# How the weights' sums of a cross attention are laid out, and who divides by them: one decoder layer on one NeuronCore

## The chip, the cores and the metric

The kernel runs on one core of one Trainium2 chip. The metric is the device time of one execution in microseconds (us). The core's engines run side by side, each through its own list of instructions in order: TensorE (PE in the profile; PEld is its loading of stationary operands), VectorE (DVE), ScalarE (ACT), GpSimd (POOL) and SyncE (SP), which issues the DMAs. They wait for each other on semaphores. TensorE writes into eight banks of PSUM (128 x 512 floats each) and the others read them.

## The reference

One layer of a decoder for x of 2048 x 256 and a context of 1601 x 256, all in float32:

```python
x = x + self_attention(layernorm(x))          # 16 heads of 16, causal, ALiBi
x = x + cross_attention(layernorm(x), ctx)    # 16 heads of 64, below
x = x + fp8_gemm(layernorm(x))                # 256 x 256
# cross attention
q, k, v = query @ Wq + bq, ctx @ Wk + bk, ctx @ Wv + bv
attn = softmax(q k^T / 8)                     # over the 1601 keys, for each head
out = concat_heads(attn @ v) @ Wo + bo + query
out = layernorm(out) * gamma + beta
```

## The kernel before, in words

A class `Order` writes one list of stages by hand; every engine's program walks through this list and does its own part of each stage. What stands later in the list comes later on every engine, and a wait of one instruction holds everything behind it on its engine. The method `after(steps, what)` puts a stage into the list a number of steps of the attention later.

The change is in the cross attention. Its 16 heads go in 8 pairs (`NP`), a pair is computed for 4 blocks of 512 queries (`NB`), and a block in 13 steps of 128 keys (`NS`; the last has 65). So there are 32 blocks and 416 steps. In a step TensorE makes the scores of both heads with keys on the partitions and queries in the row (L842 and L846), ScalarE writes their exponentials, the weights, from PSUM to SBUF (L1001), and TensorE multiplies them with the values (L857): head 0 into partitions 0 to 63 and head 1 into 64 to 127 of one bank, so `products` holds head, feature x query. The two heads' matmuls of a step stand one behind the other and use different columns of the array. The weights are kept in 12 buffers, six steps' worth.

The softmax needs the sum of the weights over all keys. GpSimd adds the 13 weight tiles of each head up into `added` (L1348, 24 additions of 128x512 a block, lagging behind the steps). Four steps after a block's end (`SUMS_LAG`) TensorE adds over the partitions: 8 matmuls, each with a 128x128 piece of `added` as the stationary operand and a column of ones moving (L868), which gives the sums as columns, queries on the partitions. VectorE takes the reciprocal of these 8 columns (L1186). Four steps later (`PROJECT_LAG`) TensorE projects the products, copied to `o_pair` by ScalarE (L1011), with Wo: per head and per 128 queries a matmul of 64 rows (L880), heads in separate banks since each still has to be divided by its own sums, four banks in all. VectorE reads them in 8 instructions of 128x256, each multiplying by the reciprocals and adding to the residual `resid` (L1204).

Beside the steps of one pair, TensorE does the work ahead for the next: projections (L664, L818) and 64 chunks of scores (L830, two banks each), from which VectorE takes the row maxima (L1107). All of this, the sums and the projection share a ring of three banks (`CROSS_RING`); `take_bank` waits until the bank used three uses ago has been read. The last pair (p = 7) has no such side work. There the tail of the layer (L1233 to L1274: the layer norms, rounding to fp8, the last product) runs between the steps, block by block, behind each block's projection (`TAIL_AT`), mostly on VectorE, with the small powers for the norms on GpSimd (L1310, L1312).

## Time and profile before

| | |
|---|---|
| median of 3 runs | 2216.82 us (2206.26 to 2250.86) |
| the profiled execution, its time | 2230.43 us |
| its span, first to last instruction | 2228.5 us |
| mean granted TensorE clock | 0.911 |
| cross attention | about 748 to the end |
| its last pair | about 2007 to the end |

The page gives each engine's busy time as a share of the span, and in 40 slices as tenths. The views behind it follow an engine in a stretch of time: what it ran, how long it sat idle before each group of instructions, and who ended that idle time.

### The profile page before, as it was taken

The numbers are of one execution on the slowest core, as the hardware profiler recorded it, in microseconds if no ns is written. First come the engines' busy times: TensorE is split into PE (matmuls) and PEld (weight loads), VectorE is DVE, ScalarE is ACT, GpSimd is POOL, SyncE is SP. The second block draws the span as 40 slices with busy tenths as digits, with TensorE's granted clock in tenths as the row PEclk, the third lists the DMA queues.
The fourth block names the chain that finished last, engine by engine and source line by source line (L and its number), as shares of the span: only waits on it lengthen the run. The fifth ranks groups of instructions, "written<-read, shape, count | busy, mean of one in ns | idle before, by whom it ended". The sixth has DMA issues, their size and how long they took to land.

```text
span 2228.5 us, 32080 instructions
## 1 busy us (share of the span) xinstructions
PE 1964.8 (88%) x11994; PEld 1069.0 (48%) x11994; DVE 1247.4 (56%) x2495; ACT 879.5 (39%) x1762; POOL 1027.2 (46%) x856
## 2 busy tenths in 40 slices
...
GB/s 103 26 31 30 30 16 17 31 92 1 11 38 29 8 1 8 1 1 10 1 1 11 1 1 11 1 1 10 1 1 3 1 1 3 1 26 3 1 19 38
DMA packets 27746, 34.63 MB, mean 16 GB/s; under 512 B 3986, under 2 KB 25811, under 8 KB 25939
## 3 DMA queue, kind: packets, MB, share of 16 engines
...
q14 instruction: 59, 0.48, 0.1%
...
## 4 chain that ended last, share of the span: by engine, by line
PE 75%; DVE 11%; issue 6%; ACT 4%; POOL 2%; SPq 1%; DMA 1%; POOLq 0%; DVEq 0%; ACTq 0%
PE psum L857 17%; PE psum L842 12%; DVE maxima L1107 7%; PE psum L830 7%; PE psum L750 7%; PE psum L664 5%; PE psum L725 5%; PE psum L698 4%; PE psum L846 4%; ACT weights_room L943 3%; PE psum L880 3%; PE psum L818 2%; PE psum L868 2%; PE psum L762 2%; PE psum L734 1%
## 5 line engine op out<-in xcount | busy, mean ns | idle before, releaser
L1107 DVE TENSOR_REDUCE maxima<-psum 128x1 f32<-128x400 f32 (+5 forms) x1664 | 882.4, 583 | 456.9 <-PE psum L830 276.9
L1348 POOL TENSOR_TENSOR parts_room<-parts_room,weights_room 128x512 f32<-128x512 f32 (+1 forms) x596 | 746.8, 1286 | 339.1 <-ACT weights_room L1001 339.0
L1001 ACT ACTIVATE weights_room<-psum 128x512 f32<-128x512 f32 (+1 forms) x694 | 370.0, 597 | 610.6 <-PE psum L846 608.7
L943 ACT ACTIVATE weights_room<-psum 128x512 f32<-128x512 f32 (+3 forms) x640 | 298.0, 535 | 253.6 <-PE psum L725 136.5
L1310 POOL TENSOR_SCALAR rstd<-meanvar 128x2 f32<-128x2 f32 (+1 forms) x24 | 6.7, 280 | 701.9 <-DVE meanvar L1057 701.9
L842 PE MATMUL psum<-stack_room,k_hi 64*128 64x512 f32 (+1 forms) x1664 | 304.0, 411 | 9.3 <-ACT weights_room L1001 7.7
L830 PE MATMUL psum<-k_hi,stack_room 64*128 64x400 f32 (+1 forms) x1024 | 254.3, 404 | 37.0 <-DVE maxima L1107 34.8
L830 PEld LDWEIGHTS psum<-k_hi,stack_room 64*128 64x128 f32 x1024 | 145.5, 189 | 215.3 <-issue 124.3
L725 PE MATMUL psum<-stack_room,stack_room 51*128 51x512 f32 (+3 forms) x640 | 203.7, 458 | 41.1 <-ACT weights_room L943 39.9
L842 PEld LDWEIGHTS psum<-stack_room,k_hi 64*128 64x128 f32 (+1 forms) x1664 | 167.8, 185 | 59.6 <-issue 29.2
L846 PE MATMUL psum<-shifts,parts_room 64*128 64x512 f32 (+1 forms) x832 | 189.8, 395 | 0.0
L842 PE MATMUL psum<-stack_room,k_lo 64*128 64x512 f32 (+1 forms) x832 | 189.8, 395 | 0.0
L698 PE MATMUL psum<-stack_room,stack_room 51*128 51x512 f32 (+3 forms) x640 | 170.3, 494 | 19.2 <-DVE maxima L1107 13.1
L857 PE MATMUL psum<-weights_room,parts_room 128*64 128x512 f32 (+1 forms) x696 | 185.0, 644 | 0.0
L857 PE MATMUL psum<-weights_room,v_pair 128*64 128x512 f32 (+1 forms) x692 | 180.9, 634 | 0.0
L750 PE MATMUL psum<-weights_room,v_self 128*32 128x512 f32 (+3 forms) x1280 | 180.4, 618 | 0.0
L1348 POOL TENSOR_TENSOR parts_room<-parts_room,parts_room 128x512 f32<-128x512 f32 (+1 forms) x118 | 148.5, 1282 | 50.4 <-ACT parts_room L1001 50.4
L725 PEld LDWEIGHTS psum<-stack_room,stack_room 51*128 51x128 f32 x640 | 98.9, 209 | 118.8 <-ACT weights_room L943 96.6
L880 PE MATMUL psum<-parts_room,parts_room 64*128 64x256 f32 x512 | 83.1, 445 | 73.0 <-DVE stack_room L1204 53.9
L1204 DVE SCALAR_TENSOR_TENSOR stack_room<-psum,parts_room,stack_room 128x256 f32<-128x256 f32 x256 | 112.1, 480 | 62.6 <-PE psum L880 60.3
L698 PEld LDWEIGHTS psum<-stack_room,stack_room 51*128 51x128 f32 x640 | 74.8, 212 | 146.1 <-issue 120.9
L1001 ACT ACTIVATE parts_room<-psum 128x512 f32<-128x512 f32 (+1 forms) x138 | 75.1, 600 | 130.8 <-PE psum L846 130.8
...
## 6 DMA issues: line engine op xcount, KB each, us to landing
...
stack_room<-shift_rows SPq DMA_DIRECT2D x64, 2.0 KB
...
```

Source lines behind the costliest of these rows:

```text
L698: last = engine.matmul(slots[m][:, 0:k1 - k0], q_stack[p % NSTACK][r, i * P:(i + 1) * P], k_stack[p % NSTACK][r, k0:k1], start=True, stop= ...
L725: last = engine.matmul(self_scores[u % SELF_SCORES][:, 0:n], k_stack[p % NSTACK][r, j * P:(j + 1) * P], q_stack[p % NSTACK][r, q0:q0 + n], ...
L750: last = engine.matmul(products[c:c + COL, q0:BQ], v_self[:, j0 + n, h * VW:h * VW + COL], w_self[(s0 + n) % NW][:, m, 0:BQ - q0], start=j ...
L830: filled(use + n, engine.matmul(slot[:, 0:k1 - k0], q_hi[p % 2][r:r + DH2, i * P:(i + 1) * P], k_hi[p % 2][r:r + DH2, k0:k1], start=True, ...
L842: engine.matmul(pair_scores[u % NSCORES][:kw, :], k[r:r + DH2, j * P:j * P + kw], q[r:r + DH2, block(b)], start=n == 0, stop=False)
L846: engine.matmul(pair_scores[u % NSCORES][:kw, :], one_row[r:r + DH2, :kw], shifts[r:r + DH2, b, :], start=False, stop=True).then_inc(pair_ ...
L857: engine.matmul(products[r:r + DH2, :], v_pair[p % 2][:kw, j, r:r + DH2], weights[u % NP_WEIGHTS][:kw, :], start=j == 0, stop=j == NS - 1) \
L880: last = [engine.matmul(slots[m][:, t * D:(t + 1) * D], o_pair[n_block % 2][m * DH2:(m + 1) * DH2, i * P:(i + 1) * P], wo2[p % 2][m * DH2: ...
L943: engine.activation(w_self[s % NW][:, m, 0:n], self_scores[(HP * s + m) % SELF_SCORES][:, 0:n], ACT.Exp, scale=SELF_SCALE).then_inc(exp_do ...
L1001: engine.activation(weights[u % NP_WEIGHTS][:kw, :], pair_scores[u % NSCORES][:kw, :], ACT.Exp, scale=CROSS_SCALE).then_inc(pair_exp, 1)
L1107: engine.tensor_reduce(maxima[:, p % 2, i // TB, n, i % TB, ch:ch + 1], bank_of(use + n)[:, 0:real - k0], AX.X, ALU.max) \
L1348: engine.tensor_tensor(sum_[:kw, m, :], old[:kw, :], new, ALU.add).then_inc(weights_added, 1)
```

## The change

1. The sums. TensorE takes 64 columns of ones as the stationary operand and moves `added`: two matmuls of 64x512, one for each head, into partitions 0 to 63 and 64 to 127 of a bank. Every partition of a head then holds that head's sums, one for each query, laid out like `products`.
2. The division. ScalarE copies this bank to `pair_recip` in SBUF, VectorE takes reciprocals in place in four instructions of 128x128, one a step (`pair_invert`), and then multiplies `o_pair` by them (`pair_divide`, 128x512).
3. The projection. With the products divided, both heads are summed within one matmul of 128 rows: 4 matmuls in 2 banks instead of 8 in 4. VectorE adds them to the residual in two instructions of 128x512. It comes 7 steps after the sums instead of 4.
4. The last pair. Head 1's weights are added by VectorE, head 0's by GpSimd as before; `added_with` counts both.

```diff
@@ -26,7 +26,7 @@
 FOLD_LAG, TURN_LAG, OUT_LAG = 2, 2, 2
-SUMS_LAG, PROJECT_LAG = 4, 4
+SUMS_LAG, PROJECT_LAG = 4, TB + 3
 SELF_RING, SELF_SCORES = 4, 3
 CROSS_RING, NSCORES = 3, 4
@@ -216,6 +216,9 @@
     def pair_sums(self, p, b):
         self.put("pair_sums", p, b, banks=1)
+        for t in range(TB):
+            self.after(t + 1, lambda t=t: self.put("pair_invert", p, b, t))
+        self.after(TB + 1, lambda: self.put("pair_divide", p, b))
         self.after(PROJECT_LAG, lambda: self.pair_out(p, b))
     def pair_sweep2(self, p):
@@ -238,7 +241,7 @@
         return steps
     def pair_out(self, p, b):
-        self.put("pair_project", p, b, banks=4)
+        self.put("pair_project", p, b, banks=2)
         if b == NB - 1 and p + 2 < NP:
             self.put("pair_out_load", p + 2)
         if p == NP - 1:
@@ -457,9 +460,17 @@
         return HP * (pair_step_of[p, b, NS - 1] + 1)
-    def added_with(p, b, j, n):
-
-        return HP * (NS - 1) * pair_finish_no[p, b] + HP * max(0, j - 1) + n + 1
+    def on_vector(p, m):
+
+        return p == NP - 1 and m == HP - 1
+
+    def added_with(p, b, j, m):
+
+        done = (NS - 1) * pair_finish_no[p, b] + max(1, j)
+        if on_vector(p, m):
+            return added_on_vector, done - (NS - 1) * NB * (NP - 1)
+        alone = (NS - 1) * max(0, pair_finish_no[p, b] - NB * (NP - 1)) + (max(1, j) if p == NP - 1 else 0)
+        return added_on_pool, HP * (done - alone) + alone - (HP - 1 - m if p < NP - 1 else 0)
     consts_set = sem("consts_set")
@@ -638,6 +650,21 @@
     def y_done(on_pool_, on_dve, b, i):
         return (on_pool_, pieces_done(b, i)) if b < NB - 1 else (on_dve, i + 1)
+
+    def add(waiting, engine, p, b, j, s, m):
+
+        n_block, kw, u = pair_finish_no[p, b], min(P, S - j * P), HP * s + m
+        sum_ = added[n_block % 2][:, m, :]
+        waiting.wait_ge(pair_exp, u + 1)
+        if j == 1:
+            if n_block >= 2:
+                waiting.wait_ge(*bank_filled(use_of[("pair_sums", *pair_finishes[n_block - 2])]))
+            old = weights[(u - HP) % NP_WEIGHTS]
+        else:
+            waiting.wait_ge(*added_with(p, b, j - 1, m))
+            old = sum_
+        engine.tensor_tensor(sum_[:kw, :], old[:kw, :], weights[u % NP_WEIGHTS][:kw, :], ALU.add) \
+            .then_inc(added_with(p, b, j, m)[0], 1)
     def tensor_program(engine):
         pe = Waiting(engine)
@@ -862,27 +889,24 @@
                 sum_ = added[pair_finish_no[at] % 2]
                 slot = take_bank(use)
                 for m in range(HP):
-                    pe.wait_ge(weights_added, added_with(p, b, NS - 1, m))
-                    for t in range(TB):
-                        n = m * TB + t
-                        last = engine.matmul(slot[:, n:n + 1], sum_[:, m, t * P:(t + 1) * P], ones_v[:, 0:1],
-                                             start=True, stop=True)
+                    pe.wait_ge(*added_with(p, b, NS - 1, m))
+
+                for m in range(HP):
+                    last = engine.matmul(slot[m * DH2:(m + 1) * DH2, :], ones_v[:, :], sum_[:, m, :], start=True,
+                                         stop=True)
                 filled(use, last)
             elif kind == "pair_project":
                 p, b = at
                 n_block = pair_finish_no[at]
-                pe.wait_ge(evicted, n_block + 1)
+                pe.wait_ge(divided, n_block + 1)
                 pe.wait_ge(wo_pair_in[p % 2], 16 * (p // 2 + 1))
                 for half in range(2):
-                    slots = [take_bank(use + HP * half + m) for m in range(HP)]
+                    slot = take_bank(use + half)
                     for t in range(HT):
                         i = HT * half + t
-                        last = [engine.matmul(slots[m][:, t * D:(t + 1) * D],
-                                              o_pair[n_block % 2][m * DH2:(m + 1) * DH2, i * P:(i + 1) * P],
-                                              wo2[p % 2][m * DH2:(m + 1) * DH2, :], start=True, stop=True)
-                                for m in range(HP)]
-                    for m in range(HP):
-                        filled(use + HP * half + m, last[m])
+                        last = engine.matmul(slot[:, t * D:(t + 1) * D], o_pair[n_block % 2][:, i * P:(i + 1) * P],
+                                             wo2[p % 2], start=True, stop=True)
+                    filled(use + half, last)
             elif kind == "tail_turn":
                 b, i = at
                 slot = take_bank(use)
@@ -994,17 +1018,21 @@
                     if u >= NP_WEIGHTS:
                         was = pair_scores_at[(u - NP_WEIGHTS) // HP]
                         act.wait_ge(pair_values_done, u - NP_WEIGHTS + 1)
-                        act.wait_ge(weights_added, added_with(*was[:3], m))
+                        act.wait_ge(*added_with(*was[:3], m))
                     else:
                         act.wait_ge(values_done, SELF_STEPS)
                     engine.activation(weights[u % NP_WEIGHTS][:kw, :], pair_scores[u % NSCORES][:kw, :], ACT.Exp,
                                       scale=CROSS_SCALE).then_inc(pair_exp, 1)
+            elif kind == "pair_sums":
+                if pair_finish_no[at]:
+                    act.wait_ge(divided, pair_finish_no[at])
+                turned(use, pair_recip)
             elif kind == "pair_finish":
                 n_block = pair_finish_no[at]
                 act.wait_ge(pair_values_done, pair_last(*at))
                 if n_block >= 2:
-                    act.wait_ge(*bank_filled(use_of[("pair_project", *pair_finishes[n_block - 2])] + 2 * HP - 1))
+                    act.wait_ge(*bank_filled(use_of[("pair_project", *pair_finishes[n_block - 2])] + 1))
                 else:
                     act.wait_ge(one_made, 1)
@@ -1178,33 +1206,32 @@
                         src = bank_of(use)[:kw, (ta - t0) * P:(tb - t0) * P].rearrange("p (t d) -> p t d", d=P)
                         last = engine.tensor_tensor(v_pair[p % 2][:kw, ta:tb, :], src, bias, ALU.add)
                 last.then_inc(emptied(use), 1)
-            elif kind == "pair_sums":
+            elif kind == "pair_scores":
+                p, b, j, s = at
+                for m in range(HP):
+                    if j and on_vector(p, m):
+                        add(dve, engine, p, b, j, s, m)
+            elif kind == "pair_invert":
+                p, b, t = at
+                cols = slice(t * P, (t + 1) * P)
+                dve.wait_ge(*bank_read(use_of["pair_sums", p, b]))
+                engine.reciprocal(pair_recip[:, cols], pair_recip[:, cols]).then_inc(inverted, 1)
+            elif kind == "pair_divide":
                 n_block = pair_finish_no[at]
-                dve.wait_ge(*bank_filled(use))
-                if n_block >= 2:
-                    dve.wait_ge(*bank_read(use_of[("pair_project", *pair_finishes[n_block - 2])] + 2 * HP - 1))
-                engine.reciprocal(pair_recip[n_block % 2].rearrange("p n t -> p (n t)"),
-                                  bank_of(use)[:, 0:HP * TB]).then_inc(emptied(use), 1)
+                dve.wait_ge(evicted, n_block + 1)
+                dve.wait_ge(inverted, TB * (n_block + 1))
+                engine.tensor_tensor(o_pair[n_block % 2], o_pair[n_block % 2], pair_recip, ALU.mult) \
+                    .then_inc(divided, 1)
             elif kind == "pair_project":
                 p, b = at
-                n_block = pair_finish_no[at]
                 dve.wait_ge(resid_biased, b + 1)
-                dve.wait_ge(*bank_read(use_of["pair_sums", p, b]))
                 for half in range(2):
-                    for m in range(HP):
-                        u = use + HP * half + m
-                        if m:
-                            dve.wait_ge(*bank_read(u - 1))
-                        elif p:
-                            dve.wait_ge(*bank_read(use_of["pair_project", p - 1, b] + HP * half + HP - 1))
-                        dve.wait_ge(*bank_filled(u))
-                        for t in range(HT):
-                            i = HT * half + t
-                            row = resid[:, TB * b + i, :]
-                            last = engine.scalar_tensor_tensor(row, bank_of(u)[:, t * D:(t + 1) * D],
-                                                               pair_recip[n_block % 2][:, m, i:i + 1], row, ALU.mult,
-                                                               ALU.add)
-                        last.then_inc(emptied(u), 1)
+                    rows = resid[:, TB * b + HT * half:TB * b + HT * half + HT, :]
+                    if p:
+                        dve.wait_ge(*bank_read(use_of["pair_project", p - 1, b] + half))
+                    dve.wait_ge(*bank_filled(use + half))
+                    engine.tensor_tensor(rows, bank_of(use + half).rearrange("p (t d) -> p t d", t=HT), rows, ALU.add) \
+                        .then_inc(emptied(use + half), 1)
             elif kind == "tail_weights":
                 dve.wait_ge(tails_in, 16 * 6)
                 engine.tensor_tensor(out_scale, scales[:, 0:1], scales[:, 1:2], ALU.mult) \
@@ -1331,21 +1358,9 @@
                         .then_inc(resid_biased, 1)
             elif kind == "pair_scores":
                 p, b, j, s = at
-                if j:
...
+                for m in range(HP):
+                    if j and not on_vector(p, m):
+                        add(pool, engine, p, b, j, s, m)
             elif kind == "tail_product" and at[0] < NB - 1:
                 b, i = at
                 pool.wait_ge(*bank_read(use))
```

How this moves instructions, at the three places of which the prediction speaks. First TensorE where a block is projected, in pair 6 (L830 is a chunk for the next pair, L846 ends a step's scores, L857 multiplies weights and values, `parts_room_88` is `wo2` and `parts_room_95` `o_pair`). Before:

```order
L846 MATMUL psum<-shifts,parts_room_98 128x512 x2
L830 MATMUL psum<-k_hi,stack_room_2_107 128x400 x2
L880 MATMUL psum<-parts_room_88,parts_room_95 128x256 x8
L857 MATMUL psum<-parts_room_101,parts_room_103 64x512
L857 MATMUL psum<-parts_room_102,parts_room_103 64x512
```

and now, where the same lines are L873, L857, L907 and L884:

```order
L873 MATMUL psum<-shifts,parts_room_98 65x512 x2
L857 MATMUL psum<-k_hi,stack_room_2_106 128x400 x2
L907 MATMUL psum<-parts_room_88,parts_room_95 128x256 x4
L884 MATMUL psum<-weights_room_60,parts_room_102 64x512
L884 MATMUL psum<-weights_room_61,parts_room_102 64x512
```

The projection stands between a chunk and value matmuls as before, three steps later in its block, with half the matmuls.

Second VectorE in one block of the same pair (maxima are the chunks' row maxima, `stack_room_7` is `resid`). Before:

```order
L1107 TENSOR_REDUCE maxima<-psum 128x1 x28
L1186 RECIPROCAL parts_room_99<-psum 128x8
L1120 TENSOR_REDUCE shift<-maxima 128x8
L1107 TENSOR_REDUCE maxima<-psum 128x1 x12
L1204 SCALAR_TENSOR_TENSOR stack_room_7_104<-psum,parts_room_99,stack_room_7_104 128x256 x8
```

and now:

```order
L1135 TENSOR_REDUCE maxima<-psum 128x1 x12
L1218 RECIPROCAL parts_room_99<-parts_room_99 128x128 x2
L1135 TENSOR_REDUCE maxima<-psum 128x1 x6
L1218 RECIPROCAL parts_room_99<-parts_room_99 128x128 x2
L1135 TENSOR_REDUCE maxima<-psum 128x1 x6
L1223 TENSOR_TENSOR parts_room_96<-parts_room_96,parts_room_99 128x512
L1135 TENSOR_REDUCE maxima<-psum 128x1 x6
L1233 TENSOR_TENSOR stack_room_7_103<-psum,stack_room_7_103 128x512 x2
```

The reciprocals come in twos, with three chunks' maxima (six reductions) behind each two.

Third VectorE in the last pair, from the rounding of a block's first half to its second half (L1076 and L1104 round, `norm_room_125` and so on are the halves' row tops). Before nothing of the sums stands there but 8 instructions of the projection behind it:

```order
L1248 TENSOR_SCALAR norm_room_115<-x_block,meanvar,rstd 128x256 x2
L1070 TENSOR_SCALAR parts_room_80<-parts_room_80 128x512
L1072 TENSOR_SCALAR parts_room_80<-parts_room_80 128x512
L1074 TENSOR_TENSOR parts_room_80<-parts_room_80 128x512
L1076 TENSOR_TENSOR norm_room_116<-parts_room_80 128x512
...
L1263 TENSOR_SCALAR norm_room_129<-norm_room_129,norm_room_124 128x2
L1070 TENSOR_SCALAR parts_room_80<-parts_room_80 128x512
...
L1204 SCALAR_TENSOR_TENSOR stack_room_7_104<-psum,parts_room_100,stack_room_7_104 128x256 x8
```

and now, from the same place on:

```order
L1275 TENSOR_SCALAR norm_room_114<-x_block,meanvar,rstd 128x256 x2
L1098 TENSOR_SCALAR parts_room_80<-parts_room_80 128x512
...
L1290 TENSOR_SCALAR norm_room_128<-norm_room_128,norm_room_123 128x2
L1218 RECIPROCAL parts_room_99<-parts_room_99 128x128
L666 TENSOR_TENSOR parts_room_93<-parts_room_93,weights_room_63 128x512
L666 TENSOR_TENSOR parts_room_93<-parts_room_93,parts_room_101 128x512
L1223 TENSOR_TENSOR parts_room_96<-parts_room_96,parts_room_99 128x512
L666 TENSOR_TENSOR parts_room_93<-parts_room_93,weights_room_55 65x512
L1098 TENSOR_SCALAR parts_room_80<-parts_room_80 128x512
```

Additions of weights (L666), reciprocals and the division now stand between the two halves' rounding, ahead of the projection's additions.

## Rows read from the trace of the kernel before

**Rows 1.** The page: busy time, and the chain that ended last.

```profile
PE 1964.8 (88%) x11994; PEld 1069.0 (48%) x11994; DVE 1247.4 (56%) x2495; ACT 879.5 (39%) x1762; POOL 1027.2 (46%) x856
...
PE 75%; DVE 11%; issue 6%; ACT 4%; POOL 2%; SPq 1%; DMA 1%; POOLq 0%; DVEq 0%; ACTq 0%
```

**Rows 2.** Stretches: us, then PE, PEld, DVE, ACT, POOL busy, PEclk, DMA, GB/s.

```profile
1050.00:1995.00 945.00, 883.27 (x5357) 508.74 (x5355) 505.50 (x1013) 348.96 (x662) 663.46 (x535) 0.97 0.01 3
...
2039.30:2069.90 30.60, 29.48 (x190) 15.53 (x190) 6.45 (x18) 13.96 (x29) 30.05 (x26) 1.00 0.00 1
2069.90:2122.00 52.10, 36.66 (x206) 18.49 (x206) 35.72 (x57) 17.52 (x36) 40.08 (x36) 0.80 0.00 1
2174.70:2202.50 27.80, 9.40 (x46) 6.58 (x47) 24.75 (x52) 3.89 (x7) 13.45 (x14) 0.56 0.12 38
```

**Rows 3.** Waits of TensorE, 1050 to 1995: total us, times, longest.

```profile
PE psum L880 <- DVE stack_room L1204: 25.2, 23, 1.1
PE psum L830 <- DVE maxima L1107: 20.7, 46, 0.5
PE psum L880 <- DVE maxima L1107: 15.6, 22, 0.8
```

**Rows 4.** Timeline of TensorE, 1723 to 1740: start, us, instructions, idle before.

```profile
1723.95 1.95 PE L868 MATMUL psum<-ones_v,parts_room 128*128 128x1 f32 x16
1725.83 1.08 PE L857 MATMUL psum<-parts_room,v_pair 128*64 128x512 f32 x4
1726.73 1.03 PE L857 MATMUL psum<-weights_room,v_pair 128*64 128x512 f32 x4
...
1734.67 0.38 PE L830 MATMUL psum<-k_hi,stack_room 64*128 64x400 f32 x2
1735.77 1.13 PE L880 MATMUL psum<-parts_room,parts_room 64*128 64x256 f32 x8 [0.72 <-DVE maxima L1107]
1738.00 1.14 PE L880 MATMUL psum<-parts_room,parts_room 64*128 64x256 f32 x8 [1.09 <-DVE stack_room L1204]
1739.07 1.51 PE L857 MATMUL psum<-weights_room,v_pair 128*64 128x512 f32 x6
```

**Rows 5.** Timeline of TensorE, 650 to 655: 8 matmuls 128x256 of 128 rows.

```profile
650.39 3.72 PE L777 MATMUL psum<-wo,o_t 128*128 128x256 f32 x16
654.04 1.06 PE L750 MATMUL psum<-weights_room,v_self 128*32 128x512 f32 x8
```

**Rows 6.** VectorE by line and form: busy us, mean ns, idle before.

```profile
L1186 DVE RECIPROCAL parts_room<-psum 128x8 f32<-128x8 f32 x32 | 6.6, 207 | 40.4 <-PE psum L868 40.4
L1213 DVE RECIPROCAL norm_room<-norm_room 128x2 f32<-128x2 f32 x1 | 0.2, 158 | 0.0
L1133 DVE TENSOR_TENSOR norm_room<-psum,recip 128x128 f32<-128x128 f32 x32 | 9.3, 291 | 1.1
L1204 DVE SCALAR_TENSOR_TENSOR stack_room<-psum,parts_room,stack_room 128x256 f32<-128x256 f32 x256 | 112.1, 480 | 62.6 <-PE psum L880 60.3
L1141 DVE TENSOR_TENSOR x_block<-psum,x_block 128x512 f32<-128x512 f32 x8 | 5.5, 692 | 43.0 <-PE psum L777 43.0
```

**Rows 7.** Timeline of VectorE, 1728 to 1736: maxima of three chunks each.

```profile
1728.18 3.27 DVE L1107 TENSOR_REDUCE maxima<-psum 128x1 f32<-128x400 f32 x6 [1.97 <-PE psum L830]
1732.84 3.26 DVE L1107 TENSOR_REDUCE maxima<-psum 128x1 f32<-128x401 f32 x6 [1.39 <-PE psum L830]
```

**Rows 8.** Timeline of VectorE and GpSimd, last pair, a rounding with and without GpSimd.

```profile
2142.59 13.99 POOL L1348 TENSOR_TENSOR parts_room<-parts_room,weights_room 128x512 f32<-128x512 f32 x10
...
2145.63 1.63 DVE L1074 TENSOR_TENSOR parts_room<-parts_room 128x512 f32<-128x512 f32 x1
...
2188.98 0.69 DVE L1074 TENSOR_TENSOR parts_room<-parts_room 128x512 f32<-128x512 f32 x1
```

**Rows 9.** Waits of TensorE and VectorE in the last pair, 2000 to the end.

```profile
PE psum L880 <- DVE stack_room L1204: 24.3, 5, 8.8
...
DVE stack_room L1233 <- POOL rstd L1312: 24.1, 4, 8.3
```

23 lines of the change are left out of this document (5 added, 18 removed).

## The prediction

> **What bounds the kernel now.** I read the page first, then busy time by stretch, then who waits for whom, then a timeline. TensorE is 88% busy and holds 75% of the chain that ended last [rows 1]. In pairs 1 to 6, 945 us, it is 883 us busy, VectorE 506 and GpSimd 663 [rows 2]: TensorE is the bound there. What it still loses it loses to VectorE, and two thirds of this stands before the projection: 25.2 us for the multiply-adds L1204 and 15.6 us for maxima, against 20.7 us before the chunks L830 [rows 3]. The timeline shows how. The projection wants four banks of a ring of three: it waits 0.72 us for the maxima of the chunk before it, runs its first half, waits 1.09 us until VectorE has emptied a bank it filled itself, and runs the second [rows 4].
>
> The last pair is different. Its second block takes 30.6 us with GpSimd busy for 30.05 and TensorE for 29.5 [rows 2]: the additions of weights are the bound, by a hair. Its third takes 52.1 us with no engine full (TensorE 36.7, VectorE 35.7, GpSimd 40.1) [rows 2]. There the engines wait in a circle: VectorE 24.1 us for the powers that stand behind the additions on GpSimd, TensorE 24.3 us for L1204 behind the tail on VectorE [rows 9].
>
> **The change, part by part.** The profiled execution took 2230.4 us, its span 2228.5; the median of the runs is 2216.8, 0.6% under it. I sum against the profile and take the same saving from the median.
>
> Of 32 blocks 28 are projected before the last pair's own (pairs 0 to 6), four in the last pair.
>
> (1) The sums. Eight matmuls take 1723.95 to 1725.83, 1.88 us. The two new ones have the shape of one step's pair of value matmuls, 128 rows by 64 columns with 512 moving, one in each half of the array, and such a pair goes from 1725.83 to 1726.73, 0.90 us, or 0.96 to the next group; I take 0.93 [rows 4]. This is on TensorE's path: 28 x 0.95 = 27 us saved. Were the two to run one after the other, about 1.86, nothing would be saved here.
>
> (2) The projection. From the moment TensorE is ready, 0.72 before 1735.77, to 1739.07 it takes 4.02 us [rows 4]. The nearest row of the new form, 128 rows by 256 columns, is 8 matmuls from 650.39 to 654.04, 0.456 each [rows 5]; four are 1.83. The first half now takes one bank and the second the next, both last read by maxima, so the wait for its own bank is gone and that for maxima nearly (0.1 left). Saved 2.1 us a block, 28 x 2.1 = 59 us. The waits alone, 40.8 us in 23 blocks [rows 3], are 1.8 of the 2.1. What is late next is the chunk that follows: it needs a bank that the new additions free, but 1.9 us of value matmuls stand between, and the additions take 0.69 each [rows 6].
>
> (3) Reciprocals. The trace has none of 128x128 in SBUF. Its two are 128x8 in 207 ns and 128x2 in 158 ns, 8.2 ns for each further column [rows 6]; at that slope 128 columns take 158 + 126 x 8.2 = 1190 ns. The low end is a pass at the speed of the 128x128 tensor_tensor, 0.29 us [rows 6]. I take 1.19, since both rows are of this very operation and no other row of VectorE costs so much a column; four a block are 4.8 us. (The Trainium skill, "VectorE: DVE Perf Modes", section "Walkthrough: the 8-slice pipeline in each mode", says that the reciprocal divides iteratively with a repeat count of 8; by it, as an estimate, 1024 cycles of 0.96 GHz, 1.07 us, come on top of the fixed part, and the case of cheap reciprocals below falls away. The slope between the two rows agrees.)
>
> What covers them is VectorE's idle time. Three chunks' maxima take 3.27 us, and two such groups start 4.66 us apart, with 1.4 to 2.0 us idle ahead of each [rows 7]. Two reciprocals stand ahead of each of two such groups. 3.27 + 2.38 = 5.65 is 1.0 us more than 4.66, and three banks are no buffer for it: the second chunk of the group needs the first one's bank. So TensorE waits 1.0 us twice a block, and the division behind it (0.69 us alone, 1.63 where GpSimd adds at that moment [rows 8]) and what else is late adds some 0.3: 2.3 us. This holds for the first three blocks of each pair, 21 of the 28. The fourth block's sums fall into the start of the next pair, where projections for the pair after stand instead of chunks, or in the last pair nothing; there the idle time covers them. Cost 21 x 2.3 = 48 us. The multiply-adds that go (8 x 0.48 = 3.8 us) and the two additions that come (1.4 us) [rows 6] stand behind the projection, where VectorE waits for TensorE; no gain of their own. ScalarE's one copy more a block is put at nothing: that engine is 349 us busy of 945 [rows 2]; without this cover it would hold the exponentials up by its own length once a block.
>
> Pairs 0 to 6: 27 + 59 - 48 = 38 us saved.
>
> (4) The last pair. Its first two blocks go from GpSimd's bound to TensorE's: 29.5 us busy, less about 1 for the sums and some overlap of the records, 27.5, so 3 us each. In the third and fourth VectorE becomes the bound. It is 35.7 us busy in one [rows 2]. Take off 4.0 for L1204 and L1186, add 4.8 of reciprocals, 1.4 of additions, and thirteen instructions with two inputs in SBUF (12 additions of weights, the division). One of that shape takes 0.69 us with GpSimd idle and 1.63 with it adding [rows 8], so they are 9 to 21 us, and the block 47 to 59. GpSimd drops 12 of its 24 additions, which shortens these and the tail's own instructions: 50 us, against 52.1 now; 2 us each. The end, where VectorE is 24.8 us busy of 27.8 [rows 2], gets longer by the reciprocals: 4.8 + 0.7 + 1.4 - 4.0 = 3, with the copy 4 us. In all 6 + 4 - 4 = 6 us saved.
>
> Sum: 44 us. 2230.4 - 44 = 2186 for a profiled execution, 2216.8 - 44 = 2173 for the median; I say 2172.
>
> **The rivals.** (B) The reciprocals cost TensorE nothing, since they are cheap (0.29 us) or fit in the idle time. For it: VectorE is idle for 46% of pairs 1 to 6 [rows 2]. Against it: 1.4 us at a place is less than 2.38. Saved 27 + 59 + 6 = 92, and with cheap reciprocals some 15 more in the last pair: 2110 to 2125. Chance 0.2.
>
> (C) No change: lateness of VectorE piles up over the two groups, the division and the projection, which now waits for the division. At 4.1 us a dense block (86/21) the saving of pairs 0 to 6 is eaten; or the two sums' matmuls run one after the other, so that the change does not shorten them, and 18 are left. 2195 to 2240. Chance 0.2.
>
> (D) Slower: VectorE becomes the bound in both parts. The mechanism is that everything it gets lands on TensorE's path: 4 x 1.19 + 1.63 = 6.4 us in each dense block, 134 us against 86, and the last pair's third and fourth block at 59 us instead of 52, with 4 at the end: 48 + 14 + 4 = 66, 2283 us. It decides from about 6.2 us a dense block on. For it: the additions on VectorE meet those on GpSimd in the same steps, released one behind the other by the same step's exponentials, and the tail's first half is held behind them. Against it: half the reciprocals' time falls on idle time that is there in every group [rows 7]. (The Trainium skill, "GPSIMD Engine Reference", section "Key points", says that GpSimd shares its SBUF interfaces with VectorE's instructions of two SBUF inputs; by that rule each of the 48 new additions collides, and the last pair is this rival's. The trace agrees, 1.63 against 0.69.) Chance 0.15.
>
> The forecast itself (A) has 0.45, with its own range of 2140 to 2205: the reciprocals' waits between 1.2 and 3.5 us a block.
>
> **The numbers.** The time is A's, 2172. The range 2110 to 2250 takes in B and C; outside lie most of D and a little of B. A measurement of this kernel tells about 2%, 44 us, from no change: 2172.5 is that bound, so A falls on both sides of it. Faster: B 0.2 and 0.25 of A, 0.45. Within 2%: 0.2 of A and most of C, 0.38. Slower: D and a little of C, 0.17.
>
> **What would show it.** In the profile after: reciprocals of 1.1 to 1.25 us; the sums' group 0.9 us long on TensorE; the projection under 2.1 us with no wait on its own bank in the middle; new waits of TensorE before the chunks for maxima, some 40 us more over pairs 0 to 6, in the two groups behind the sums; blocks one and two of the last pair at 27 to 28 us, three and four near 50. It is wrong if the reciprocals last a third of that (B), if the chunks wait 4 us or more a block (C, D), or if the last pair moves by more than 20 us either way, which my sum has no term for.

## The result, and the profile after

| | before | changed |
|---|---|---|
| median of the runs, us | 2211.5 (4 runs) | 2129.2 (4 runs) |
| ratio, 95% interval | | 0.959 (0.953 to 0.965) |
| profiled execution, us; span | 2230.4; 2228.5 | 2105.8; 2104.0 |
| first block's finish to the end | 1427.8 | 1336.7 |

The change made the kernel 4.1% faster: some 90 us, where 44 were forecast. Executions that a lower granted clock lengthened are left out of the ratios, though not of the medians; the profiles of e6, e9, e10, e14 and e16 are of such executions, but from the first cross block's finish on e16's took as long as e15's, of the same program, within 0.1 us. The self-attention ahead is the same code, yet its length differs with the granted clock, from 767 us in the changed kernel's profile to 848 in e6's. Profiles are therefore compared from the first cross block's finish (ScalarE's copy of its products) on. "Pairs 0 to 6" runs from that finish to the same one of pair 7: 1238.6 us before and 1165.8 after, 72.8 less. "Last pair" is the rest: 189.2 and 171.0, 18.2 less.

The page after, busy time and chain, against [rows 1]:

```profile
PE 1869.7 (89%) x11354; PEld 995.6 (47%) x11354; DVE 1359.7 (65%) x2479; ACT 896.9 (43%) x1794; POOL 982.9 (47%) x808
...
PE 72%; DVE 18%; ACT 5%; issue 3%; SPq 1%; DMA 1%; POOL 1%; ACTq 0%; POOLq 0%; DVEq 0%
```

TensorE still bounds it; VectorE's share of the chain grew from 11% to 18%.

Stretches after: pairs 1 and 2, then the last pair's second and third block (us, then PE, PEld, DVE, ACT, POOL busy, clock, DMA, GB/s):

```profile
980.19:1136.41 156.22, 151.38 (x890) 84.41 (x892) 97.22 (x172) 65.78 (x125) 121.13 (x97) 1.00 0.02 4
1136.41:1300.33 163.92, 154.16 (x890) 85.62 (x892) 103.14 (x172) 65.78 (x125) 120.67 (x97) 0.98 0.02 4
...
1933.04:1962.57 29.53, 28.50 (x170) 13.91 (x172) 22.16 (x23) 14.52 (x30) 19.45 (x16) 1.00 0.00 1
1962.57:2007.44 44.87, 33.51 (x178) 16.83 (x180) 40.06 (x66) 16.92 (x34) 25.29 (x23) 0.89 0.00 1
```

The same work, pairs 1 and 2, took 7.7 us more in the second. VectorE is busy for 5.9 us more there with the same 172 instructions, so one of them lasted longer. Before, pairs 1 and 5:

```profile
1028.69:1201.42 172.73, 161.81 (x970) 92.76 (x972) 90.06 (x180) 63.44 (x120) 119.33 (x97) 0.96 0.01 4
...
1716.93:1885.09 168.16, 157.29 (x970) 91.47 (x972) 90.07 (x181) 63.44 (x120) 119.32 (x97) 0.99 0.01 2
```

Here VectorE's busy time is the same in both and only the clock differs, by 4.6 us of length.

TensorE after, sums (L895) and projection (L907), against [rows 4]:

```profile
1664.73 1.08 PE L895 MATMUL psum<-parts_room,ones_v 128*64 128x512 f32 x4
1665.64 1.89 PE L884 MATMUL psum<-weights_room,v_pair 128*64 128x512 f32 x8
...
1686.98 1.97 PE L907 MATMUL psum<-parts_room,parts_room 128*128 128x256 f32 x8
1688.88 1.51 PE L884 MATMUL psum<-weights_room,v_pair 128*64 128x512 f32 x6
```

From start to the next group's start the sums take 0.91 us and the projection 1.90, with no wait inside. VectorE after, reciprocals and what follows:

```profile
1672.12 1.76 DVE L1218 RECIPROCAL parts_room<-parts_room 128x128 f32<-128x128 f32 x2
1673.79 1.95 DVE L1135 TENSOR_REDUCE maxima<-psum 128x1 f32<-128x400 f32 x4
```

Two take 1.76 us, 0.88 each.

**The division** is one instruction of 0.68 us where GpSimd is idle. In pairs 1 to 6 the second blocks and nearly all fourth ones give 1.6 us. The first and third ones give 0.83 to 0.88 or, five times, 4.5 to 7.0. Each of the shorter ones ends 0.55 us after the addition of GpSimd that ran when it began: 0.3 us of that addition were left for those of 0.86, 1.1 us for those of 1.6. The same place in pairs 1 and 2, VectorE:

```profile
1002.96 0.86 DVE L1223 TENSOR_TENSOR parts_room<-parts_room,parts_room 128x512 f32<-128x512 f32 x1
...
1159.18 6.99 DVE L1223 TENSOR_TENSOR parts_room<-parts_room,parts_room 128x512 f32<-128x512 f32 x1
```

GpSimd and TensorE around the second:

```profile
1155.69 9.92 POOL L666 TENSOR_TENSOR parts_room<-parts_room,weights_room 128x512 f32<-128x512 f32 x8
...
1166.70 0.70 PE L857 MATMUL psum<-k_hi,stack_room 64*128 64x400 f32 x1 [5.04 <-DVE maxima L1135]
1167.33 3.78 PE L907 MATMUL psum<-parts_room,parts_room 128*128 128x256 f32 x8
```

GpSimd's unbroken row of additions ends at 1165.61, the division 0.56 us later; the chunk's maxima stand behind it, and TensorE waits 5.04 us for them. Its clock then falls to half (us, busy times, clock):

```profile
1163.00:1165.00 2.00, 0.00 (x0) 0.00 (x0) 2.00 (x1) 0.00 (x0) 2.00 (x3) 0.99 0.00 0
1165.00:1167.00 2.00, 0.30 (x1) 0.28 (x1) 2.00 (x3) 0.00 (x0) 0.61 (x1) 0.50 0.00 0
1167.00:1169.00 2.00, 2.00 (x5) 1.40 (x5) 1.09 (x3) 0.00 (x0) 0.00 (x0) 0.50 0.00 0
```

0.50 is the level of 1.2 GHz: the projection behind the wait takes 3.71 us instead of 1.90. Before, the same fall stood behind the projection's two waits. TensorE before:

```profile
1352.72 1.14 PE L880 MATMUL psum<-parts_room,parts_room 64*128 64x256 f32 x8 [0.76 <-DVE maxima L1107]
1354.95 1.59 PE L880 MATMUL psum<-parts_room,parts_room 64*128 64x256 f32 x8 [1.09 <-DVE stack_room L1204]
```

and its clock there, in stretches:

```profile
1355.00:1357.00 2.00, 2.00 (x10) 1.11 (x12) 1.20 (x4) 0.00 (x0) 1.50 (x2) 0.62 0.00 0
1357.00:1359.00 2.00, 2.00 (x8) 0.47 (x4) 1.26 (x3) 0.00 (x0) 0.00 (x0) 0.53 0.26 66
```

In stretches of 1 us there are 15 such falls in pairs 1 to 5 before, 50 us at half clock (so about 25 us lost), behind the projection or behind the sums' 1-column matmuls, and four after, 20 us, behind the long divisions there (the fifth long one stands in pair 6). Over pairs 0 to 6 it is 90 us before and 51 after.

### The profile page after: what moved, and what is told of

It reads as the page before. It is cut to its first block, busy times and chain, and to the rows that moved or that the text cites. A ratio compares the mean times of both kernels' runs of the same rounds, so it can differ in the third digit from the quotient of the medians.

```text
span 2104.0 us, 30713 instructions
## 1 busy us (share of the span) xinstructions
PE 1869.7 (89%) x11354; PEld 995.6 (47%) x11354; DVE 1359.7 (65%) x2479; ACT 896.9 (43%) x1794; POOL 982.9 (47%) x808
## 4 chain that ended last, share of the span: by engine, by line
PE 72%; DVE 18%; ACT 5%; issue 3%; SPq 1%; DMA 1%; POOL 1%; ACTq 0%; POOLq 0%; DVEq 0%
PE psum L869 14%; PE psum L884 13%; DVE maxima L1135 8%; PE psum L857 6%; PE psum L777 6%; PE psum L691 5%; PE psum L752 4%; PE psum L873 4%; PE psum L725 4%; ACT weights_room L967 4%; PE psum L907 3%; PE psum L845 3%; DVE parts_room L1223 2%; DVE parts_room L1218 2%; PE psum L789 2%
## 5 line engine op out<-in xcount | busy, mean ns | idle before, releaser
L666 POOL TENSOR_TENSOR parts_room<-parts_room,weights_room 128x512 f32<-128x512 f32 (+1 forms) x558 | 708.8, 1301 | 236.1 <-ACT weights_room L1025 233.1
L857 PE MATMUL psum<-k_hi,stack_room 64*128 64x400 f32 (+1 forms) x1024 | 261.8, 401 | 53.7 <-DVE maxima L1135 51.4
L857 PEld LDWEIGHTS psum<-k_hi,stack_room 64*128 64x128 f32 x1024 | 147.4, 187 | 225.6 <-issue 115.1
L752 PE MATMUL psum<-stack_room,stack_room 51*128 51x512 f32 (+3 forms) x640 | 194.8, 436 | 43.3 <-ACT weights_room L967 41.6
L873 PE MATMUL psum<-shifts,parts_room 64*128 64x512 f32 (+1 forms) x832 | 195.7, 398 | 0.0
L725 PE MATMUL psum<-stack_room,stack_room 51*128 51x512 f32 (+3 forms) x640 | 160.1, 466 | 20.5 <-DVE maxima L1135 14.1
L884 PE MATMUL psum<-weights_room,parts_room 128*64 128x512 f32 (+1 forms) x696 | 174.3, 610 | 0.0
L884 PE MATMUL psum<-weights_room,v_pair 128*64 128x512 f32 (+1 forms) x692 | 171.7, 606 | 0.0
L777 PE MATMUL psum<-weights_room,v_self 128*32 128x512 f32 (+3 forms) x1280 | 167.4, 578 | 0.0
L666 POOL TENSOR_TENSOR parts_room<-parts_room,parts_room 128x512 f32<-128x512 f32 (+1 forms) x111 | 143.3, 1311 | 22.5 <-ACT parts_room L1025 22.1
L752 PEld LDWEIGHTS psum<-stack_room,stack_room 51*128 51x128 f32 x640 | 93.4, 197 | 118.8 <-ACT weights_room L967 97.9
L725 PEld LDWEIGHTS psum<-stack_room,stack_room 51*128 51x128 f32 x640 | 70.2, 199 | 136.9 <-issue 111.2
L1218 DVE RECIPROCAL parts_room<-parts_room 128x128 f32<-128x128 f32 x128 | 112.5, 920 | 0.0
L873 PEld LDWEIGHTS psum<-shifts,parts_room 64*128 64x128 f32 (+1 forms) x832 | 104.2, 184 | 15.0 <-issue 0.6
```

The source lines that it names most:

```text
L666: engine.tensor_tensor(sum_[:kw, :], old[:kw, :], weights[u % NP_WEIGHTS][:kw, :], ALU.add) \
L725: last = engine.matmul(slots[m][:, 0:k1 - k0], q_stack[p % NSTACK][r, i * P:(i + 1) * P], k_stack[p % NSTACK][r, k0:k1], start=True, stop= ...
L752: last = engine.matmul(self_scores[u % SELF_SCORES][:, 0:n], k_stack[p % NSTACK][r, j * P:(j + 1) * P], q_stack[p % NSTACK][r, q0:q0 + n], ...
L777: last = engine.matmul(products[c:c + COL, q0:BQ], v_self[:, j0 + n, h * VW:h * VW + COL], w_self[(s0 + n) % NW][:, m, 0:BQ - q0], start=j ...
L857: filled(use + n, engine.matmul(slot[:, 0:k1 - k0], q_hi[p % 2][r:r + DH2, i * P:(i + 1) * P], k_hi[p % 2][r:r + DH2, k0:k1], start=True, ...
L873: engine.matmul(pair_scores[u % NSCORES][:kw, :], one_row[r:r + DH2, :kw], shifts[r:r + DH2, b, :], start=False, stop=True).then_inc(pair_ ...
```

## The experiments

Theory, after the first look: the reciprocals are short and hidden, sums and projection save what was forecast and some clock besides, and GpSimd's row takes part of it back through the division. The rival: the reciprocals cost 2.3 us a block as forecast, and the other parts saved far more than was summed. All ratios are against the kernel before, run on the same chip.

**e1, no reciprocals.**
```diff
-        for t in range(TB):
-            self.after(t + 1, lambda t=t: self.put("pair_invert", p, b, t))
...
```
(The division then waits for ScalarE's copy instead.)


> The changed kernel without its 128 reciprocals; the products are multiplied by the sums themselves, everything else stays. Theory 1 (the reciprocals are short, 0.88 us, and run under the value matmuls of two steps, so they cost TensorE 0.2 us each time): the dense blocks get 0.4 to 0.6 us shorter each, some 12 us over pairs 0 to 6, and the last pair, where VectorE is busiest, some 5: about 17 us under the changed kernel, 2100 to 2108. Theory 2 (they cost what the prediction said, 2.3 us a dense block, and sums and projection saved more than was summed): 48 us and 7 in the last pair, about 2065. Theory 3 (they cost nothing at all anywhere): 2115 to 2121, as the changed kernel.

Ratio 0.955 (0.949 to 0.962); last pair 166.7 us. Its pairs without a long division take 155.1:

```profile
988.98:1144.10 155.12, 150.48 (x890) 84.00 (x892) 85.73 (x156) 65.78 (x125) 121.20 (x97) 1.00 0.02 4
```

156.22 against 155.12: four blocks' reciprocals cost 1.1 us, 0.3 a block, and 4.3 us in the last pair (which differs by up to 1.6 us between three profiles of the changed kernel). Theory 2's 2065 is out. The ratio alone can't tell 1 from 3; the pair can.

**e2, the sums alone, in the kernel before.**
```diff
-                    for t in range(TB):
-                        n = m * TB + t
-                        last = engine.matmul(slot[:, n:n + 1], sum_[:, m, t * P:(t + 1) * P], ones_v[:, 0:1],
+                for m in range(HP):
+                    last = engine.matmul(slot[m * DH2:(m + 1) * DH2, :], ones_v[:, :], sum_[:, m, :], start=True,
...
```


> The kernel before with the sums alone as two matmuls of 64 stationary ones by 512 moving; the reciprocals stay small and so read another layout, and the division is not the right one. Theory 1: the group goes from 1.88 to 0.91 us, so 28 x 0.97 = 27 us less, and the last pair 1 to 3: about 2182. Theory 2 (the sums saved more than their own length, since the reciprocals start earlier or a bank comes free earlier): 2160 to 2170. If VectorE's lateness takes it back: no difference, 2205 to 2212.

0.983 (0.978 to 0.987). Pairs 0 to 6 take 49.6 us less, nearly twice the 27 of 28 blocks' matmuls. The rest is clock: 44 us at half clock instead of 90, 23 us. A pair at full clock takes 162.7:

```profile
1181.87:1344.55 162.68, 151.76 (x922) 84.19 (x924) 89.91 (x180) 63.44 (x121) 119.32 (x97) 1.00 0.01 4
```

The last pair didn't move (190.4). The saving in the profiles, 48 us from the first finish to the end, is Theory 2's size; by the ratio it is 38 us (28 to 49), between the two theories. The clock was named by neither.

**e3, the projection alone, in the kernel before.**
```diff
-        self.put("pair_project", p, b, banks=4)
+        self.put("pair_project", p, b, banks=2)
...
-                                              o_pair[n_block % 2][m * DH2:(m + 1) * DH2, i * P:(i + 1) * P],
-                                              wo2[p % 2][m * DH2:(m + 1) * DH2, :], start=True, stop=True)
-                                for m in range(HP)]
+                        last = engine.matmul(slot[:, t * D:(t + 1) * D], o_pair[n_block % 2][:, i * P:(i + 1) * P],
+                                             wo2[p % 2], start=True, stop=True)
...
```


> The kernel before with the projection alone changed: four matmuls of 128 rows in two banks instead of eight of 64 rows in four, head 0's reciprocals used for both heads, so half of the 256 multiply-adds L1204 go as well. Theory 1 (projection 4.02 to 1.9 us, its own bank's wait gone): 28 x 2.1 = 59 us less in pairs 0 to 6, and in the last pair 10 to 15, since the wait of 24 us on L1204 [rows 9] stands in the middle of the projection and goes with the four banks: 2137 to 2143. Theory 2 (pairs 0 to 6 save only the wait of 1.09 and the shorter matmuls reappear as waits before the chunks; the last pair gains from VectorE's additions and not from here): 28 x 1.1 = 31 us, about 2180.

0.960 (0.952 to 0.968): by itself as much as the whole change. Pairs 0 to 6 take 83.7 us less: 28 x 2.1 = 59, and half clock for 37 us instead of 90, 27. The last pair takes 171.5, 17.7 less, with every addition on GpSimd. TensorE's 24.3 us of waits for L1204 within the projection are gone (10.5 us stand before the tail's turn instead), and VectorE's for the powers are 14.1 us instead of 24.1. Theory 1, and more.

**e4, the changed kernel with all additions on GpSimd.**
```diff
-        return p == NP - 1 and m == HP - 1
+        return False
```
(and the count that `added_with` gives, to suit.)


> The changed kernel with both heads' weights added on GpSimd in the last pair too, as before. Pairs 0 to 6 stay as they are. Theory 1 (the last pair's 19.5 us came mostly from the two-bank projection that breaks the circle of waits, and VectorE's additions gave and took): within 5 us of the changed kernel either way, 2116 to 2126, the first two blocks 3 us longer each as GpSimd is the bound there again, the next two shorter by as much. Theory 2 (it came from the additions on VectorE): 12 to 20 us longer, 2133 to 2141, the third and fourth block each 6 to 8 longer. Theory 3 (the forecast's picture of VectorE as the bound in the third and fourth block): 5 to 15 us shorter than the changed kernel.

0.971 (0.964 to 0.978), about 26 us over the changed kernel. The last pair took 192.2 us; its second block:

```profile
1953.35:1996.27 42.92, 30.92 (x170) 15.19 (x172) 31.54 (x22) 14.52 (x30) 34.18 (x30) 0.84 0.00 0
```

and VectorE in it, one division:

```profile
1964.50 22.28 DVE L1222 TENSOR_TENSOR parts_room<-parts_room,parts_room 128x512 f32<-128x512 f32 x1
```

Theory 2 is nearest: the last pair is 21 us longer, a little over its 12 to 20. But 13 of them are in the second block, with the long division, which was in no theory, and only 3.6 and 4.7 in the third and fourth. Pairs 0 to 6, the same code as in the changed kernel, took 12.7 us more, with seven long divisions instead of five. This run turned the study to the division.

**e5, an instruction of one SBUF input in the division's place.**
```diff
-                engine.tensor_tensor(o_pair[n_block % 2], o_pair[n_block % 2], pair_recip, ALU.mult) \
+                engine.tensor_scalar(o_pair[n_block % 2], o_pair[n_block % 2], 0.5, None, ALU.mult) \
```


> The changed kernel with the division replaced by an instruction of the same size with one SBUF input (products times a constant), so that only the number of SBUF inputs changes; the values are not divided. In the changed kernel the division takes 0.83 to 0.88 us, 1.62 to 1.65, and five times 4.5 to 7.0, each time until GpSimd's unbroken row of additions ends, and TensorE waits up to 5.0 us behind it. Theory 1 (two SBUF inputs make VectorE's instruction wait for a gap on GpSimd): all 32 last under 0.8 us, TensorE's waits of over 2 us are gone, every pair from 1 to 5 takes 155 to 157 us instead of up to 163.9, and the time is 20 to 30 us under the changed kernel, 2092 to 2102. Theory 2 (the long ones are long for another reason: a wait that stands in the record, SBUF traffic, or the step at which they stand): they stay, and the time is within 5 us of the changed kernel.

0.953 (0.947 to 0.959). Three of 28 are long still. VectorE:

```profile
1321.82 6.70 DVE L1223 TENSOR_SCALAR parts_room<-parts_room 128x512 f32<-128x512 f32 x1
...
1948.67 0.41 DVE L1223 TENSOR_SCALAR parts_room<-parts_room 128x512 f32<-128x512 f32 x1
```

So the number of SBUF inputs is not what counts. This form takes 0.41 us alone, faster than the 0.68 of tensor_tensor, and waits for GpSimd as well. The additions L1233, with one input in PSUM and one in SBUF, took 0.69 us in all of pairs 1 to 5, and the reciprocals 0.92 us, whatever GpSimd did. The Trainium skill, "SBUF — State Buffer", section "Who interferes with whom", has both: two SBUF inputs contend with a GpSimd instruction that reads SBUF, and tensor_scalar can enter a mode that uses the shared ports; one SBUF input outside these modes does not. The traces agree with that. It also says that whoever issues first has the shared pair for the whole of its instruction while the other is blocked. The shorter divisions agree, as they end 0.55 us after the one addition that ran (0.28 us for tensor_scalar). The long ones waited for more than one instruction: they end as long after the last addition of the row, three or five additions further on in the pairs and seventeen in e4.

**e6, the division on GpSimd** (the block `elif kind == "pair_divide"` moved from VectorE's program to GpSimd's).


> The changed kernel with the division on GpSimd, in its own order between its additions; a full result. Theory 1: no instruction of VectorE in pairs 0 to 6 then meets GpSimd's stream; the division takes one addition's time, about 1.3 us, and TensorE's waits behind it are gone; pairs 1 to 5 take 155 to 158 us, about 20 us under the changed kernel, 2096 to 2106, and in the last pair GpSimd's additions come 1.3 us later per block. Theory 2 (GpSimd, 120 of 156 us busy in a pair, is late, and the projection waits for it, or its additions hold up the exponentials): no gain or a loss, 2120 to 2140.

0.987 (0.980 to 0.994): Theory 2, and worse. Each of pairs 1 to 5 takes 170.7 us. Waits of TensorE, pairs 1 to 5 (us in all, times, longest):

```profile
PE psum L907 <- POOL parts_room L1362: 42.2, 20, 3.0
```

All 20 projections wait for it, 2.1 us each, and the clock falls too (0.96).

**e7, each reciprocal twice.**
```diff
+                chain.on(engine.reciprocal(pair_recip[:, cols], pair_recip[:, cols]))
+                after_last()
                 engine.reciprocal(pair_recip[:, cols], pair_recip[:, cols]).then_inc(inverted, 1)
```
(`after_last` makes the second wait for the first.)


> The changed kernel with each of the 128 reciprocals made twice, one behind the other, so that the sums themselves stand there again and the division is not the right one. It tests the prediction's rule for the cover: stall at each of two places a block = 3.27 of maxima + the reciprocals there - 4.66. Theory 1 (the rule holds, only the 1.19 us in it was too much): two at a place are 1.75 us and cost 0.36, four are 3.5 and cost 2.1; 21 dense blocks x 2 x 1.75 more = 73 us, and 4 x 3.5 in the last pair = 14 at most: 2190 to 2210. Theory 2 (the value matmuls of 1.9 us and the three banks cover more than the rule says): half of that or less, 2140 to 2165.

1.019 (1.011 to 1.026), slower than the kernel before. Pairs 0 to 6: 106.8 us more than the changed kernel, the last pair 14.9. Half clock for 125 us instead of 51 is 37 of the 106.8. But no division is longer than 1.8 us here, so that the 21 us of waits behind the changed kernel's five long ones are gone, and some 91 us are left for the reciprocals, where the rule has 73; the other 18 are not explained. The wait of TensorE behind the first two reciprocals of pair 1's second block shows the rule itself. The changed kernel, e1 and e7:

```profile
1031.36 0.45 PE L857 MATMUL psum<-k_hi,stack_room 64*128 64x402 f32 x1 [0.67 <-DVE maxima L1135]
...
1039.58 0.45 PE L855 MATMUL psum<-k_hi,stack_room 64*128 64x402 f32 x1 [0.49 <-DVE maxima L1133]
...
1069.50 0.45 PE L857 MATMUL psum<-k_hi,stack_room 64*128 64x402 f32 x1 [2.66 <-DVE maxima L1135]
```

In pairs 1 to 5 of e7 there are 31 waits for maxima of 1.0 to 2.7 us, 2.1 on average, as the rule says. So for four reciprocals at a place the rule holds, with a bill for the clock on top that puts the time above Theory 1's range. A small overrun costs little where 2 us is ruinous.

**e8, VectorE's additions alone, in the kernel before** (`on_vector`, `added_with` and `add` of the change, nothing else).


> The kernel before with only the last pair's additions of one head's weights moved to VectorE. Before, the last pair (from its first block's finish to the end) took 189.2 us; with the projection alone changed 171.5; in the changed kernel 171.0, and 192.2 with all additions on GpSimd, where one division took 22.3 us. Theory 1 (the additions on VectorE help the changed kernel because they break GpSimd's unbroken row, on which the division waits; without a division there is only the tail's rounding that gains): 0 to 8 us less than before, 2204 to 2212. Theory 2 (they relieve a GpSimd that is the bound in itself): blocks one to four 5 to 8 us shorter each, 20 us in all, about 2190. Theory 3 (collisions of the 48 new instructions cost more than they save): 5 to 20 us longer.

0.998 (0.994 to 1.001); the last pair takes 183.0, 6.2 less. Theory 1.

**e9, GpSimd waits for the division.**
```diff
+            elif kind == "pair_divide":
+                pool.wait_ge(divided, pair_finish_no[at] + 1)
```


> The changed kernel with one wait more on GpSimd: at the step of the division it waits until VectorE has divided, so that its row of additions has a gap there. Theory 1 (the division can start only when GpSimd's row breaks; the form with one SBUF input waited as well, so it is the access that both engines share, not the number of inputs): all divisions then last under 1 us, none of 4.5 to 7.0, TensorE's waits of 2.7 to 5.0 us and the half clock behind them are gone, pairs 1 to 5 take 155 to 157 us each against 161.1 on average, so 20 to 25 us under the changed kernel: 2095 to 2102. The last pair stays at 170. Theory 2 (the wait moves the lateness to GpSimd, as the division on GpSimd did, whose pairs took 170.7): 165 to 171 us a pair, 2150 to 2185.

0.955 (0.947 to 0.963). The longest divisions are 4.5 us instead of 7.0, six of 28 are still long, and pairs 1 to 5 take 160.7 to 166.2. The gap is there but late: GpSimd is some additions behind. Neither theory as written.

**e10, the same wait with all additions on GpSimd.** The edits of e4 and e9.


> The same wait in the kernel with both heads' weights added on GpSimd in the last pair. There the last pair took 192.2 us, with one division of 22.3 us, against 171.0 with one head's additions on VectorE and 171.5 with only the projection changed. Theory 1 (the additions on VectorE helped by breaking GpSimd's row): with the gap given in another way the last pair takes 172 to 178, so it is nearly as good as with them. Theory 2 (they helped by taking work off a GpSimd that is the bound): 185 to 192 still.

0.963 (0.953 to 0.973), last pair 185.0. One division still lasts 17.7 us, until GpSimd's late row ends. Inconclusive: the gap came too late to test what it was made for.

**e11, one reciprocal of 128x512.**
```diff
-        for t in range(TB):
-            self.after(t + 1, lambda t=t: self.put("pair_invert", p, b, t))
+        self.after(1, lambda: self.put("pair_invert", p, b, 0))
...
```


> The changed kernel with one reciprocal of 128x512 in place of four of 128x128. By two reciprocals in 1.75 us the column costs about 5.7 ns over a fixed 0.15, so one takes 3.0 to 3.1 us. Doubling the reciprocals made pairs 1 to 5 14 us longer each (175.5 against 161.1), with 3.5 us of them at each of two places a block. Theory 1 (what counts is how much stands at one place against the cover there): 3.1 at one place costs about 1.3 to 2.5 us a block in three blocks a pair, 4 to 8 us a pair, 2140 to 2165. Theory 2 (the reciprocals' total counts, which falls by 0.4 us a block): no longer than the changed kernel, 2115 to 2125.

```profile
L1217 DVE RECIPROCAL parts_room<-parts_room 128x512 f32<-128x512 f32 x32 | 107.0, 3343 | 0.0
```

0.963 (0.956 to 0.970). 3.34 us, so (3343 - 920) / 384 = 6.3 ns for each column. Its pairs take 161.1 to 162.8 with no division over 1.7 us, against 156.2: 5 us a pair for less reciprocal time in all. Theory 1.

**e12, the division one step earlier; e13, one step later; e14, the changed kernel again.**
```diff
-        self.after(TB + 1, lambda: self.put("pair_divide", p, b))
+        self.after(TB, lambda: self.put("pair_divide", p, b))
```
(e13 has `TB + 2` there, and e14 no edit.)


> The changed kernel with the division one step earlier, right behind the fourth reciprocal and ahead of the chunk's maxima instead of behind them. In the changed kernel the divisions of each pair's first and third block find GpSimd in a row of additions that lasts 4.0 to 6.9 us more; most start within it (0.83 to 0.88 us), but five of 28 do not and last until the row ends (4.5 to 7.0). Theory 1 (whether a division gets in hangs on its place within GpSimd's addition: those with 0.42 to 0.61 us of the current one left got in, those with 0.23 to 0.31 did not): moved by some 3 us, another place, the same for all blocks of a kind, so that either none is long (pairs 155 to 157, 2095 to 2105) or nearly all of a kind are (pairs 165 to 172, 2140 to 2180). Theory 2 (it is a matter of chance wherever it stands): again about one in five long, pairs of 156 and of 161 to 164 mixed, 2110 to 2125.

> The changed kernel with the division one step later. As for the kernel with the division earlier: by Theory 1 all of a kind are short (2095 to 2105) or nearly all long (2140 to 2180); by Theory 2 about one in five is long, 2110 to 2125. The projection follows one step behind it, so a loss of up to 1 us a block, 20 us, is possible from a projection that waits for the division.

> The changed kernel itself once more, beside the two with the division moved. Theory 1: 2115 to 2125, and a profile in which again a few of the 14 divisions of first and third blocks last 4.5 us or more, though not the same ones. If the same five are long again, the place in the program sets it, not the fine timing.

e12: 0.964 (0.955 to 0.973). One division of 28 is long, the others of pairs 0 to 6 take 0.96 to 1.20 us; but three instructions, 2.9 us, now stand ahead of a chunk's maxima, and pairs 2 to 5 take 163.9. So the place counts, but not as its Theory 1 has it: in the three profiles that follow, the short divisions of first and third blocks of pairs 1 to 6 began 0.25 to 0.34 us before the end of the running addition and the long ones 0.27 to 0.36, which does not separate them. e13 gave, instruction for instruction on every engine, the changed kernel again: no instruction stands between the two steps. So there are three profiles of one program. Five, five and seven of 28 divisions are long, and not the same ones: that of pair 1's first block took 0.86, 0.82 and 6.98 us. All stand in a pair's first or third block. The place says which divisions are at risk, small timing which of them lose. The cross phase is 1336.7, 1338.5 and 1348.5 us. e14's ratio was 0.951 (0.940 to 0.962); e13 has none.

**e15, GpSimd waits a step earlier; e16, two steps earlier.**
```diff
+            elif kind == "pair_invert" and at[2] == 3:
+                pool.wait_ge(divided, pair_finish_no[at[:2]] + 1)
```
(e16 has `at[2] == 2`.)


> The changed kernel with GpSimd waiting for the division as in the kernel whose GpSimd waits, but one step earlier in its own order, at the fourth reciprocal. There GpSimd was up to three additions late when the division came, and the long divisions lasted 4.5 us instead of 7.0. Theory 1 (a division starts at the latest when GpSimd's row breaks, and GpSimd has 35 us of slack in a pair of 156 to give one): two additions fewer stand before the gap, the long ones last 2 us at most, TensorE's waits of over 2 us and the half clock behind them go, pairs 1 to 5 take 155 to 158, 2095 to 2108. Theory 2 (GpSimd is late enough already that a gap holds up the sums or the exponentials): pairs of 160 to 168, 2115 to 2150, with waits of TensorE or ScalarE for GpSimd's additions.

> As the one before, two steps earlier. Theory 1: four additions fewer before the gap, so no division meets GpSimd at all (0.69 us each); GpSimd idles up to 5 us a block, 20 of its 35 us of slack; the time as the one before or up to 10 us longer. Theory 2: its lateness costs 10 us a pair, 2160 and more.

The two are again one program, as no addition stands between the steps. 0.951 (0.944 to 0.957) and 0.944 (0.936 to 0.952); the cross phase took 1295.6 us in both profiles, 41 under the changed kernel's and 132 under that of before. A pair, and the divisions of pairs 1 to 5:

```profile
1160.65:1316.40 155.75, 151.30 (x890) 84.30 (x892) 95.08 (x173) 65.78 (x125) 119.34 (x97) 1.00 0.02 4
```
```profile
L1223 DVE TENSOR_TENSOR parts_room<-parts_room,parts_room 128x512 f32<-128x512 f32 x20 | 13.6, 681 | 0.0
```

GpSimd there (start, us, idle before):

```profile
1179.97 2.52 POOL L666 TENSOR_TENSOR parts_room<-parts_room,weights_room 128x512 f32<-128x512 f32 x2
1184.17 2.51 POOL L666 TENSOR_TENSOR parts_room<-parts_room,weights_room 128x512 f32<-128x512 f32 x2 [1.67 <-DVE parts_room L1223]
```

GpSimd gives up 1.7 us in the first and third block of a pair and 2.8 in the others, every division takes 0.68, all five pairs 155.7 to 155.8 at full clock. Theory 1: the row was the cause, and breaking it is worth about 41 us of the cross phase. In pairs 0 to 6 it is 38.7 us: the 21 us of waits behind long divisions, and 17 for 34 us less at half clock. This version beats the kernel before by the ratio, and the changed kernel by the profiles; the whole times, with the self-attention's differences in them, lie the same way, but the intervals of the ratios (0.951 and 0.944 against 0.959 and e14's 0.951) overlap.

## Why the prediction was wrong

The sign and the bound were right, the size was not: 44 us forecast, some 90 measured, nearly the 92 of rival B. Three terms make the difference: VectorE's cost (48 forecast, some 28 measured), the clock (none forecast, some 20 gained), and the last pair (6 forecast, 18 measured).

**Step (1), sums: right.** 0.91 us against 0.93. **Step (2), projection: right.** 1.90 us against 1.83 and 0.1, and its own bank's wait is gone. But both were taken at full clock only. (28 blocks' sums and projections stand in pairs 0 to 6, as forecast: 27 and 59 us.)

**Step (3) failed, in its size: "Cost 21 x 2.3 = 48 us".** The reciprocal takes 0.88 us, not 1.19. The slope of 8.2 ns a column came from two short forms of which one reads PSUM and one SBUF; over 128 and 512 columns in SBUF it is 6.3. (The estimate from the repeat count of 8 that the Trainium skill, "VectorE: DVE Perf Modes", section "Walkthrough: the 8-slice pipeline in each mode", gives for the reciprocal was 1.07 us and a fixed part on top; the trace does not agree with it either.) With 1.75 us in place of 2.38 the cover rule leaves 3.27 + 1.75 - 4.66 = 0.36 us, so a quarter off the duration takes two thirds off the stall; at 3.5 e7 bears it out. The count of places was wrong too: not two in each of three blocks, but three a pair, two behind the second block's reciprocals and one behind the fourth's, which the forecast took as covered. TensorE waits 0.67 to 0.82 us there against 0.48 without reciprocals (e1). Measured: 0.3 us a block, some 7 us over pairs 0 to 6.

**The division was priced at 1.63 at most, from [rows 8]: wrong.** That row showed one length of a wait that has several. Five long ones cost 5.0 us of wait twice and 3.8 three times, 21 us, and half clock behind each.

**The clock was no term of the sum.** 39 us less at half clock over pairs 0 to 6 is about 20 us; the waits that the forecast took away were also what made it fall. Pairs 0 to 6 summed anew: 27 + 59 + 20 - 7 - 21 = 78, against 72.8 measured and 38 forecast. 5 us stay unexplained.

**Step (4), last pair: 18.2 us saved, 6 forecast.** The third and fourth block took 44.9 each instead of the 50 expected, the second 29.5, not 27.5, and the end got 2.2 shorter, not 4 longer. VectorE was near its bound (40.1 of 44.9), but not at 47 to 59: its additions took 1.2 us on average, not up to 1.63. e3 shows that the gain is from the projection, which breaks the circle of waits [rows 9]; e8 that VectorE's additions give 6 by themselves; e4 that in the changed kernel they are worth 21, 13 of them since they keep a division from meeting a long row. The division is in this pair's path as well, which the sum left out. TensorE in the last pair after:

```profile
PE psum L907 <- DVE parts_room L1223: 16.9, 4, 6.2
```

**Rivals.** B had the time and part of the reason: the reciprocals nearly fit, though not at 0.29 us. That its 92 meets the 91 measured is luck: it has neither the 28 us that VectorE cost nor the 32 that the clock and the last pair gave beyond it. D's collisions exist: the Trainium skill, "GPSIMD Engine Reference", section "Key points", says that VectorE's instructions with two SBUF inputs contend with GpSimd, and the trace agrees, with 1.2 us on average for an addition that has 0.69 alone. But that is below the 1.63 on which D rested. D's bound of 6.2 us a dense block, (86 + 44) / 21, leaves out its own 18 us in the last pair; with them it is 5.3.
